# Three PSUM evacuations written by VectorE instead of ScalarE, and a batch's first q projection placed one segment later, in a fused attention and MLP kernel

## The reference

```
x = x + attn(layernorm(x)) ;  x = x + ffn(layernorm(x))
attn: qkv = x @ W_qkv ; scores = q k^T / 8 + slope * (pos_k - pos_q), causal
      out = softmax(scores) @ v ; return out @ W_out
ffn:  P = x @ U1 ; H = gelu(P @ V1 + b1) ; Q = H @ U2 ; return Q @ V2 + b2
```

## Time and profile before

| | before |
|---|---|
| time, median of 3 runs | 2795.6 us (2795.47 to 2796.94) |
| profiled execution, own time | 2801.86 us |
| its span in the trace | 2800.1 us |
| mean granted TensorE clock | 0.989 of full |
| TensorE busy | 2679.7 us (96%) |
| ScalarE busy | 2172.2 us (78%) |
| GpSimd busy | 1999.2 us (71%) |
| VectorE busy | 1992.2 us (71%) |

### The profile page before, as it was taken

One profiled execution on the slowest core, in us unless ns is written; L12 is line 12 of the kernel. 1 busy time (PEld: TensorE's weight loads), 2 busy tenths in 40 slices (PEclk: granted clock), 3 DMA queues, 4 the chain that ended last, 5 costly groups with the idle time before them and its releaser, 6 DMA issues.

```text
span 2800.1 us, 83228 instructions
## 1 busy us (share of the span) xinstructions
PE 2679.7 (96%) x31112; PEld 1836.7 (66%) x31112; DVE 1992.2 (71%) x6795; ACT 2172.2 (78%) x3892; POOL 1999.2 (71%) x1816
## 2 busy tenths in 40 slices
PE   4999999999999999999999999999999999999986
PEld 1577666666666667666676766667666666666663
DVE  6667677676777767677776777767677776776753
ACT  3777878778787887878878788887878878788783
POOL 1677777777777777777777777777777777777784
PEclk9999999999999999999999999999999999999997
DMA  6445444444444444444454444544454454544421
GB/s 170 93 101 94 94 94 93 89 100 88 97 93 95 96 88 98 91 101 90 92 100 87 97 94 96 94 90 96 94 97 90 92 98 87 99 92 94 93 50 31
DMA packets 486951, 260.76 MB, mean 93 GB/s; under 512 B 309770, under 2 KB 484874, under 8 KB 486282
## 3 DMA queue, kind: packets, MB, share of 16 engines
q1 hardware_dynamic: 486548, 255.43, 44.2%
HBM read 27.73 MB, written 8.39 MB: 13 GB/s over the span
## 4 chain that ended last, share of the span: by engine, by line
PE 71%; ACT 10%; issue 7%; POOL 6%; DMA 3%; DVE 2%; SPq 1%; ACTq 0%; POOLq 0%; DVEq 0%
PE proj L486 33%; PE scores L486 18%; PE o_acc L486 12%; PE max_scores L486 7%; POOL p_lo L1164 4%; ACT p_f L785 3%; ACT p_hi L744 2%; ACT L785 2%; ACT h_f L877 2%; DMA o_t<-o_hi_lo 2%; POOL h_lo L1194 1%; DVE xn_t_lo L904 1%; DMA q_operands<-neg_max_t_lo 1%; PE proj L639 1%; ACT xn_t_hi L744 1%
## 5 line engine op out<-in xcount | busy, mean ns | idle before, releaser
L1164 POOL TENSOR_TENSOR p_lo<-p_f,p_hi 128x512 f16<-128x512 f32 x1280 | 1481.3, 1170 | 743.7 <-ACT p_hi L744 742.7
L977 DVE CUSTOM_DVE_ANT_0 max_scores<-max_scores,causal 128x512 f32<-128x512 f32 (+3 forms) x2048 | 969.4, 507 | 289.2 <-PE max_scores L486 279.5
L785 ACT ACTIVATE p_f<-scores 128x512 f32<-128x512 f32 x1280 | 754.4, 589 | 156.1 <-PE scores L486 140.8
L744 ACT ACTIVATE p_hi<-p_f 128x512 f16<-128x512 f32 x1280 | 800.2, 625 | 14.2
L486 PE MATMUL scores<-q_operands,k_lo_hi 128*128 128x512 f16 (+3 forms) x2048 | 614.7, 300 | 22.3 <-ACT p_f L785 17.8
L486 PE MATMUL scores<-q_operands,k_hi_aug 128*128 128x512 f16 (+3 forms) x2048 | 586.8, 299 | 0.0
L486 PE MATMUL o_acc<-v_hi_one,p_lo 128*128 128x65 f16 x5120 | 518.1, 194 | 11.8 <-POOL p_lo L1164 10.9
L486 PE MATMUL o_acc<-v_hi_one,p_hi 128*128 128x65 f16 x5120 | 517.9, 194 | 0.0
L486 PE MATMUL o_acc<-v_lo,p_hi 128*128 128x64 f16 x5120 | 517.3, 193 | 0.0
L486 PE MATMUL max_scores<-k_hi_aug,q_operands 96*128 96x512 f16 (+3 forms) x2048 | 491.2, 301 | 14.6 <-DVE row_max L977 10.2
L486 PEld LDWEIGHTS o_acc<-v_hi_one,p_lo 128*128 128x128 f16 x5120 | 471.6, 98 | 46.3 <-POOL p_lo L1164 27.7
(11 more groups left out here) (126 smaller groups left out, 4293.7 us busy)
## 6 DMA issues: line engine op xcount, KB each, us to landing
q_operands<-q_pair_hi SPq DMA_DIRECT2D x512, 128.0 KB, 2.5
q_operands<-q_pair_lo SPq DMA_DIRECT2D x512, 64.0 KB, 2.1
k_hi_aug<-k_pair_hi SPq DMA_DIRECT2D x256, 64.0 KB, 2.0
k_lo_hi<-k_pair_hi SPq DMA_DIRECT2D x256, 64.0 KB, 2.0
k_lo_hi<-k_pair_lo SPq DMA_DIRECT2D x256, 64.0 KB, 2.0
x_rows<-in_L_attn_inputs SPq DMA_DIRECT2D x17, 512.0 KB, 4.1
x_acc<-in_L_attn_inputs SPq DMA_DIRECT2D x64, 128.0 KB, 2.4
out<-x_rows SPq DMA_DIRECT2D x16, 512.0 KB, 3.2
```

The lines of the kernel that those rows point to most:

```text
L744: return nc.scalar.activation(out_ap, in_ap, ACT.Copy, scale=scale)
L785: nc.scalar.activation(p_f[:, k % 3, :], score_bank[k % 2][:, :], ACT.Exp).then_inc(exp_done, 1)
L977: last = nc.vector.tensor_tensor_reduce(out=bank, in0=bank, in1=causal[:, (T - 1 - qt) * P:S], scale=1.0, scalar=-3e38, op0=ALU.add, op1=A ...
L1164: nc.gpsimd.tensor_tensor(p_lo[:, slot, n, :], p_f[:, k % 3, :], p_hi[:, slot, n, :], ALU.subtract).then_inc(lo_p, 1)
```

## The change

Three evacuations move from ScalarE to VectorE. The high half of v in steps 1 and 3 and the high half of q in step 13 are written by VectorE with a tensor_scalar (a multiplication by the same constant, from PSUM), directly in front of the low half that VectorE writes anyway; new semaphores `hi_v_dve` and `hi_q_dve` say when they are done. Apart from that, `q_segment(0)` becomes 2 instead of 1. TensorE then issues q(0) one segment later, and ScalarE's and VectorE's halves of it and SP's four DMAs follow, since they are placed by `q_segment` too.

```diff
 def q_segment(s):
-    return 2 if s % 2 else 1
+    return 2 if s % 2 or s == 0 else 1
+DVE_V, DVE_Q = (1, 3), (13,)
...
+def act_before(s, on_dve, places):
+    return len([at for at in places if at <= s and at not in on_dve])
+V_STEPS = [s for s in range(KV) if s % 8 < 4]
+def high_count(i, s, on_dve, places):
+    if s in on_dve:
+        return i.value() * len(on_dve) + on_dve.index(s) + 1
+    return i.value() * (len(places) - len(on_dve)) + act_before(s, on_dve, places)
...
-                        sp.wait_ge(hi_q, at(g + 1))
+                        sp.wait_ge(hi_q_dve if s in DVE_Q else hi_q, high_count(i, s, DVE_Q, range(KV)))
...
-                        if n == q_segment(s) + 1 and mode in (FIRST, MID):
+                        if n == q_segment(s) + 1 and s not in DVE_Q and mode in (FIRST, MID):
                             high_q(s)
...
-                        if n == V_SEG and s % 8 < 4 and mode in (FIRST, MID):
+                        if n == V_SEG and s in V_STEPS and s not in DVE_V and mode in (FIRST, MID):
...
+                def high_v(sv):
+                    t, half = sv % 8, sv // 8
+                    dve.wait_ge(pe_v, at(i * 8 + half * 4 + t + 1))
+                    if 2 * (i * KV + (0 if half else -8)) > 0:
+                        dve.wait_ge(pe_av, at(2 * (i * KV + (0 if half else -8))))
+                    nc.vector.tensor_scalar(v_hi[:, t, half * 8:(half + 1) * 8, 0:HD],
+                                            proj("v", sv)[:, :].rearrange("p (k d) -> p k d", d=HD),
+                                            KV_OUT, None, ALU.mult).then_inc(hi_v_dve, 1)
+                def high_q(s):
+                    g = i * KV + s
+                    dve.wait_ge(pe_q, at(g + 1))
+                    landed = Q_DMAS * 16 * (2 * i + (s - 2) // RING + 1)
+                    if landed > 0:
+                        dve.wait_ge(qdup_in[(s - 2) % RING], at(landed))
+                    nc.vector.tensor_scalar(qs[0][:, s % 2, :], proj("q", s)[:, :], Q_OUT, None, ALU.mult).then_inc(hi_q_dve, 1)
...
-                            dve.wait_ge(hi_v, at(i * 8 + half * 4 + t + 1))
+                            if sv in DVE_V:
+                                high_v(sv)
+                            dve.wait_ge(hi_v_dve if sv in DVE_V else hi_v, high_count(i, sv, DVE_V, V_STEPS))
...
-                            dve.wait_ge(hi_q, at(g + 1))
+                            if s in DVE_Q:
+                                high_q(s)
+                            dve.wait_ge(hi_q_dve if s in DVE_Q else hi_q, high_count(i, s, DVE_Q, range(KV)))
```

More of the change, by code:

```diff
@@ L306, in layer @@
         hi_q, hi_k, hi_v, hi_o, hi_m = sem("hi_q"), sem("hi_k"), sem("hi_v"), sem("hi_o"), sem("hi_m")
+        hi_q_dve, hi_v_dve = sem("hi_q_dve"), sem("hi_v_dve")
         hi_ln1, hi_ln2, hi_pp, hi_qf = sem("hi_ln1"), sem("hi_ln2"), sem("hi_pp"), sem("hi_qf")
```

## The result

| | before | after |
|---|---|---|
| time, median of 4 runs each, same chip | 2796.3 us | 2828.3 us (2826.2 to 2830.2) |
| profiled execution, own time | 2801.86 us | 2826.2 us |
| its span | 2800.1 us | 2824.3 us |
| its mean granted TensorE clock | 0.989 | 0.985 |

The change made the kernel slower: the ratio is 1.0107, with a 95% interval of 1.0092 to 1.0122. That is 32 us where 15 were forecast, and outside the range of 2804 to 2816 us. The direction was right; half of the size was missing.

The account below looks back on a forecast made before the run. TensorE, 96% busy, was taken as the bound, so only its waits count. The moved q(0) at 14.9 us, v at 0.3 and q of step 13 at 0 made 2795.6 + 15.2 = 2810.8 us, range 2804 to 2816 us.

Parts of the forecast that it names:

- The move's own price: At (0, 1), q(0) no longer covers the wait for the fifth `p_lo`; TensorE 1.03 us later per batch.
- The part's sum of 14.9 us: Cost of q(0) one segment later: 14.4 us over batches 2 to 15 plus 0.52 us in batch 1.
- Nothing takes this back in the same batch: After the moved q(0), TensorE's later waits hang on its own k projections, so the 1.03 us delay stays.
- the third rival: Slower, but by less: a later wait in the batch absorbs part of the 1.03 us; at a half, 2803.4 us; 8%.
- 14 batches at 1.03 us are 14.4 us: Batches 2 to 15, behind the moved q(0): each loses 1.03 us of TensorE time, 14.4 us in all.
- q of step 13 on VectorE: Step 13: VectorE loses nothing and nobody can use ScalarE's 0.47 us gain, as GpSimd is the limit; 0 us.
- the second rival: No change: the relief of ScalarE in step 13 pays 0.83 us in 15 batches, 12 us; 2798.4 us; 8%.
- the fourth rival: VectorE and GpSimd collide at step 13's tensor_scalar: 15 x 0.27 = 4 us, 2815 us, or 2818 us; 12%.
- The first rival: Faster: the fifth `p_lo` comes 2 us earlier, so only the removed wait before q(0) counts; 13 us, 2782.6 us; 6%.

Follow-up runs that it names:

- e1: The kernel after without the three evacuations on VectorE, so only q(0) is one segment later; 2825.3 us, ratio 1.0089 to the kernel before.
- e3_fill: The kernel after plus 12 unused matmuls of 252 columns in front of `attend` at (0, 1); 2814.7 us, ratio 1.0049 to the kernel before.
- e7_fill_4: The kernel after plus 4 unused matmuls of 252 columns in front of `attend` at (0, 1); 2815.1 us, ratio 1.0056 to the kernel before.
- e8_wait_in_before: The kernel before with VectorE writing the second `xn_t_lo` late, after extra repeated writes, TensorE's order unchanged; 2831.2 us, ratio 1.0110.
- e2_dve_only: The kernel after with q(0) back in its old segment, only the three evacuations on VectorE; 2801.0 us, ratio 1.0002 to the kernel before.
- e6_after_earlier: The kernel after with ScalarE's x halves ahead of its o halves and VectorE's `normalise` of (15, 1) earlier; 2805.9 us, ratio 1.0020 to before.
- e4_earlier_chain: The kernel before with ScalarE's x halves ahead of its o halves and VectorE's `normalise` of (15, 1) earlier; 2791.3 us, ratio 0.9964.

## Why the prediction was half right

- **The move's own price was right.** "TensorE stands still for 1.96 us in place of 0.93 us", and from (0, 3) on "1.03 us later": batch 5 is 1.04 us longer, and `attend` starts 7.61 us behind the transposes. The part's sum of 14.9 us is what the two filled kernels measure at full clock, 14.5 and 14.7 us. "Nothing takes this back in the same batch" holds too, so the third rival is out.
- **The step that failed is the one that priced a standstill by its length alone**: "14 batches at 1.03 us are 14.4 us". That sum has no term for TensorE's clock. A matmul list behind a wait was costed at the durations of the trace before, and in 7 to 11 batches it ran at 1.2 GHz for 3.4 us: 0.91 us of `attend` became 1.61. The missing term is some 8 x 1.6 = 13 us. With it the sum is 28 us; `e1` measured 25 us where its count of 7 gives 26. Of the first measurement's 32 us some 4 stay unexplained, while its two profiled executions differ by 24.2 us, where the counts give 26.1 (14.9 + 7 x 1.6). `e3_fill` and `e7_fill_4` take it away by adding work, `e8_wait_in_before` brings it without the move.
- **The trace before held the warning.** It has the very wait that the change brings into every batch: behind the last batch, at (0, 1), where there is no q(0) to cover it, `attend` waits 1.78 us for the fifth `p_lo`, and 0.9 us later the clock is at half for 3.4 us:
```profile
2683.76 0.20 PE L486 MATMUL o_acc<-v_hi_one,p_lo 128*128 128x65 f16 x1 [1.78 <-POOL p_lo L1164]
```
```profile
2684.70:2688.10 3.40, 3.40 (x28) 2.32 (x25) 1.61 (x7) 2.18 (x4) 3.13 (x4) 0.50 0.41 80
```
  The mean clock of 0.989 pointed there too: the 1.1% that is missing was never looked for. Most of it lies in the first 100 us and in the last 60, where TensorE waits most, as the window over the last 40 us shows:
```profile
2760.00:2800.00 40.00, 19.38 (x76) 8.00 (x76) 16.86 (x32) 10.02 (x18) 13.65 (x15) 0.63 0.04 14
```
  A change that doubles a wait of TensorE needed a rival by which the clock falls there too, with a price of half of the time spent low. The Trainium skill (TensorE: Matmul & The Clock Gate, HAM oscillation — how this bites in real kernels) puts the penalty of a throttled stretch at its length times 1 - 1.2/2.4; for 3.4 us that gives an estimate of 1.7 us, and the batches here show 1.6 to 1.7 (1.4 in `e8_wait_in_before`).
- **q of step 13 on VectorE: 0, right.** Both waits of TensorE in batch 7 stand as they were in the earlier trace rows, 0.33 and 0.18 us where 0.32 and 0.17 stood, so the second rival is out; `e2_dve_only` says the same in time.
```profile
1319.78 0.28 PE L505 MATMUL scores<-q_operands,k_lo_hi 128*128 128x256 f16 x1 [0.33 <-ACT p_f L804]
1324.92 0.20 PE L505 MATMUL o_acc<-v_hi_one,p_lo 128*128 128x65 f16 x1 [0.18 <-POOL p_lo L1204]
```
- **The collision of the fourth rival did not come.** The tensor_scalars from PSUM take 694 and 686 ns, against 0.68 us assumed; the groups by line and shape:
```profile
L1035 DVE TENSOR_SCALAR v_hi_one<-proj 128x512 f16<-128x512 f32 x32 | 22.2, 694 | 34.2 <-PE proj L505 34.2
L1045 DVE TENSOR_SCALAR q_pair_hi<-proj 128x512 f16<-128x512 f32 x16 | 11.0, 686 | 0.0
```
  GpSimd's two `h_lo` beside the one of step 13 take 2.28 us, against 2.26 in the earlier trace rows, and over the whole span its `p_lo` takes a mean of 1171 ns after and 1170 before. Of the two rules of the Trainium skill that the prediction cites, these rows agree with the one on PSUM operands (VectorE: DVE Perf Modes, Why PSUM operands drop a tier); the lock by a tensor_scalar (SBUF — State Buffer, Who interferes with whom) shows in no row here.
- **The first rival** (`p_lo` comes earlier by itself) is out: in batch 7 the fifth `p_lo` starts 1175.02 - 1168.62 = 6.40 us behind the transposes, where it was 1167.48 - 1161.09 = 6.39. The wait for it was not new, as the prediction had it, but came 14 more times, with the 1.8 us it named.
- **Still open:** why the low clock shows in some batches and not in others of the same execution, though all of them wait 1.79 us; the 4 us of the first measurement that the two terms leave; why the kernel before took 4 us more in the later sets; the 14.3 us between `e6_after_earlier` and `e4_earlier_chain`; and which of the two moves of `e4_earlier_chain` carries its gain, since they were not tried apart.

## What to carry to other kernels

Price a new or longer wait of TensorE twice, by its length and by what the matmuls behind it cost at half clock, and look in the trace before at where the granted clock is below 1.00 and how long TensorE had waited there. Look above all for the place where the wait already stands uncovered, be it once at the end. Where a wait brings the clock down, it can be worth shortening by a few tenths of a microsecond (1.79 to 1.36 or 1.63 us here), even with work that nobody needs. When an order is to be changed for TensorE's sake, see first which work covers which wait: q(0) looked like one that waits, and was the cover for a longer wait behind it.

## What the runs showed of the hardware

- A stretch at 1.2 GHz followed a standstill of 1.79 to 1.95 us on a TensorE that is otherwise busy on both sides (in batch 7 for 5.77 of the 7.70 us up to 1176.40, nearly all of the rest being that standstill, and for all of the time behind it). It came in 7 to 11 of 14 batches, and in none of 14 with 1.63 us or less. The length alone does not decide: behind the last batch the same wait of 1.78 to 1.79 us stands in eight traces and brought the clock down in three of them (before, `e3_fill`, `e7_fill_4`), and a wait of 2.57 us at 2717.39 of the kernel before passed at full clock. In the rows of batch 7 it lasted 3.4 us, although TensorE was busy for all of it, and cost 1.6 us.
- Twelve matmuls of 252 columns, of which nothing is used, made a kernel of 2825 us 10 us faster.
- A tensor_scalar of 128 x 512 from PSUM in fp32 to fp16 takes VectorE 686 to 694 ns, the same as a scalar_tensor_tensor from there (684 to 691). The two GpSimd operations beside one of them took 2.28 us, against 2.26 without.
